# Channel attention: eight queries' exponentials made by ScalarE alone, with their keys innermost in memory, and the maxima formed in PSUM

## The chip, the cores and the metric

The kernel runs on one core of one Trainium2 chip. The metric is device time in microseconds for one launch, which works through all four batch elements. The engines are TensorE (PE, with its weight loads shown apart as PEld), VectorE (DVE), ScalarE (ACT), GpSimd (POOL) and SyncE (SP, which here only issues DMAs).

## What is computed

Four transformer layers follow one another on x of shape 4 x 512 x 128, each an attention and a feed-forward, each with a residual and a LayerNorm. The change touches the fourth attention, which attends over channels inside each token. For every token and each of 16 heads there are 64 queries, 64 keys and 64 values, all of them scalars:

```
Q = (x @ Wq + bq).reshape(b, s, 16, 64) / 8
K, V = the same from Wk, Wv (no scale)
scores = einsum('bshq,bshk->bshqk', Q, K)        # one product per (query, key)
scores = where(k > q, -inf, scores)              # causal over channels
w = softmax(scores, axis=-1)
attn = einsum('bshqk,bshk->bshq', w, V)
out = attn.reshape(b, s, 1024) @ Wo + bo
```

So a token has 16 x 64 x 64 / 2 scores and no matmul can make them. The first layer's feed-forward matters only because its weights (w1, w2, h1, h2, w3, 2.9 MB in all) move in memory.

## The kernel before, in words

Tokens lie on the 128 partitions, 128 of them at a time, so a batch element has four token tiles (`NT`). A loop runs the four batch elements; in each the channel stage comes seventh of eight and works through the four tiles one after the other. In it the 64 queries stand in reverse order (the last query, which sees all keys, first), and are cut into half 0 (the first 32 positions) and half 1 (the last 32).

The scores of a tile are cut into chunks of up to 2048 columns (`score_chunks`), each made of pieces of four keys by some queries by 16 heads, the head innermost. A tile has 20 chunks (`NC`): six of half 1 (`EARLY`), eight of half 0 with keys 0 to 31 (the rectangle), six of half 0 with keys 32 to 63. Chunk c of a tile is "step c" below. Each chunk passes through the engines in turn:

- POOL multiplies queries by keys (L1251) into one of five buffers `D3`;
- DVE subtracts the maximum of each query (`subtract`, L1287);
- ACT takes the exponential in place (L1235);
- PE adds the exponentials over keys by transposing each key's block onto an accumulating PSUM bank (`sum_keys`, L1170), the denominator `psD`;
- DVE multiplies the exponentials by the values into one of two buffers `W3` (`weigh`, L1300), and PE sums these too, the numerator `psA`.

The order of each engine is written out by hand. DVE's step n is: whatever is due at that step, then `subtract(n + 2)`, then `weigh(n)`. PE's step n is: the denominator of chunk n, then the numerator of chunk n-1. `weigh(n)` waits for the numerator of chunk n-2, since there are two buffers `W3`. What is due at certain steps on DVE: `scan_keys` (L1269, running maxima and minima over the keys of the next tile), `maxima` (L1278 to L1280, which turns these into the maximum of each query, since a score is a product of two scalars), `finish` (reciprocal L1308 and product L1312 of a half), `residual` (L1320). PE fills queries and keys of the next tile into one bank (`fill_qk`, L1141 and L1142), ACT moves them to SBUF (`move_qk`, L1222), and for keys writes a second, head-major copy (L1226). In the first tile of a batch element nothing of this is hidden.

Of the kernel before, what the change touches and what calls it, by code (L numbers as in the profile page):

```python
# [12 lines left out]
P = 128  # L13
BATCH, T = 4, 512
NT = T // P
HID = 512
# [15 lines left out]
CHUNK = 2048  # L32


def score_chunks():

    def triangle(k0):
        out, at = [[]], 0  # L40
        for j in range(0, HD // 2, KB):
            n = HD // 2 - j
            if at + KB * NH * n > CHUNK:
                out.append([])
                at = 0
            out[-1].append((k0 + j, KB, n, at))
            at += KB * NH * n
        return out

    early = [(1, c, True) for c in triangle(0)]  # L50
    rect = [(0, [(k, KB, HD // 2, 0)], False) for k in range(0, HD // 2, KB)]
    late = [(0, c, True) for c in triangle(HD // 2)]
    return early + rect + late


def transformer(nc, inp, out, last_stage=8):
    ctx = ExitStack()
    with ctx:
# [20 lines left out]
        w1_0 = sb("w1_0", HID)  # L79
        w2_0 = sb("w2_0", HID)  # L80
        wh_0 = [sb(f"wh{j}_0", NM * HID) for j in (1, 2)]
        w3_0 = sb("w3_0", NM * P)
# [36 lines left out]
        AR = 24576  # L119
        arena = sb("arena", AR)  # L120
        top = [0]

        def take(cols):
            a = arena[:, top[0]:top[0] + cols]
            top[0] += cols
            assert top[0] <= AR, top[0]
            return a


# [23 lines left out]
        TK = take(16)  # L153

# [21 lines left out]
        QX = take(NH * HD // 2)  # L176
        QN = take(NH * HD // 2)
        RD = QX
        AT = [take(NH * HD) for _ in range(2)]
        D3 = [take(CHUNK) for _ in range(5)]  # L180
        W3 = [take(CHUNK) for _ in range(2)]

# [21 lines left out]
        chunks = score_chunks()  # L204

# [15 lines left out]
        with nc.Block() as block:  # L221
# [16 lines left out]
            def _(act):  # L238
# [6 lines left out]
                load(w1_0[:], inp["L0_ffn_w1_w"])  # L245
                load(w2_0[:], inp["L0_ffn_w2_w"])
                for w, name in zip(wh_0, ("h1", "h2")):
                    load(tiles(w[:], HID), inp[f"L0_ffn_{name}_w"].rearrange("(k p) n -> p k n", p=P))
                load(tiles(w3_0[:]), inp["L0_ffn_w3_w"].rearrange("(k p) n -> p k n", p=P))
# [30 lines left out]
            def _(pool):  # L280
# [9 lines left out]
                pool.wait_ge(consts, 7 + NE)  # L290
# [55 lines left out]
            def _(pe):  # L346
                pe.wait_ge(consts, 12 + NE)
# [47 lines left out]
        w_in = [sem(f"w_in{j}") for j in range(NSLOT)]  # L395

# [9 lines left out]
        c3 = {k: sem(f"c3_{k}") for k in ("d", "e", "w", "den", "num", "attn", "proj", "qk", "qk_sb", "v", "kh", "prod", "chain", "rT")}  # L406
# [686 lines left out]
        EARLY = sum(ch[0] == 1 for ch in chunks)  # L1093
        LATE = next(c for c in range(EARLY, NC) if chunks[c][2])

        QK_AT = {EARLY + 1 + j: j for j in range(4)}
        LAG = 1
        PROJ_AT = EARLY + 5
        V1_AT = 3
        V0_AT = LATE + 2  # L1100
        FINISH_1, FINISH_0 = EARLY + 2, 2
        RESIDUAL, SCAN, MAX_1, MAX_0 = PROJ_AT + 1, PROJ_AT + 2, PROJ_AT + 3, NC - 2
        assert MAX_1 < MAX_0 and V0_AT < NC and FINISH_0 + 1 < EARLY

        def half_of(n):
            return chunks[n % NC][0]

        def pieces(n):
            return chunks[n % NC][1]

        def filled(n):
            k, nk, w, at = pieces(n)[-1]
            return at + nk * NH * w
# [5 lines left out]
        def keys_on(a, piece):  # L1119

            k, nk, w, at = piece
# [3 lines left out]
        def queries_on(a, piece):  # L1125

            k, nk, w, at = piece
            return a[:, 0:NH * w][:, None, :].to_broadcast([P, nk, NH * w])

        def qk_bank(tt, j):  # L1130
            return psum[:, 4 + j, :] if tt == 0 else scratch

        def fill_qk(pe, tt, j):

            ps = qk_bank(tt, j)
            w, row, c = (wq3, wk3)[j // 2], 32 * (j // 2), slice(j % 2 * 512, j % 2 * 512 + 512)
            if tt > 0:
                pe.wait_ge(c3["qk_sb"], 4 * tt + j)
                if j == 3:
                    pe.wait_ge(c3["kh"], 2 * tt + 1)  # L1140
# [17 lines left out]
        def sum_keys(ps, buf, n):  # L1158


            half, ragged = chunks[n % NC][0], chunks[n % NC][2]
            first_key = 0
            last_key = HD // 2 - 1 if half == 1 else HD - 1
            for k, nk, w, at in pieces(n):
                for j in range(nk):
                    seen = w - j if ragged else w
                    for f in range(0, seen, 8):
                        rows = NH * min(8, seen - f)
                        c = at + NH * (j * w + f)
                        last = nc.tensor.matmul(ps[half][0:rows, f * NH:f * NH + P], buf[:, c:c + rows], ident[:],  # L1170
                                                start=k + j == first_key and f == 0,
                                                stop=k + j == last_key and f + 8 >= seen,
                                                is_transpose=True, skip_group_check=True)
# [40 lines left out]
        def channel_act(act):  # L1214
# [14 lines left out]
            for j in range(4):  # L1229
                move_qk(0, j)  # L1230
# [258 lines left out]
```

## Time and profile before

| | |
|---|---|
| median of 3 runs | 4073.07 us (4064.61 to 4074.36) |
| the profiled execution's own time | 4083.43 us |
| its span in the trace | 4081.8 us |
| granted TensorE clock, mean | 0.878 of full speed |
| busy share: PE, DVE, ACT, POOL | 78%, 66%, 35%, 40% |

The profiled execution has 1.6 us around its span and lies 0.25% above the median. A busy share over the whole span mixes eight stages with different limits, so the stage is read by itself in the rows below. A granted clock of 1.00 is 2.4 GHz and 0.50 is 1.2 GHz.

### The profile page before, as it was taken

The numbers are of one execution on the slowest core, as the hardware profiler recorded it, in microseconds if no ns is written. First come the engines' busy times: TensorE is split into PE (matmuls) and PEld (weight loads), VectorE is DVE, ScalarE is ACT, GpSimd is POOL, SyncE is SP. The second block draws the span as 40 slices with busy tenths as digits, with TensorE's granted clock in tenths as the row PEclk, the third lists the DMA queues.
The fourth block names the chain that finished last, engine by engine and source line by source line (L and its number), as shares of the span: only waits on it lengthen the run. The fifth ranks groups of instructions, "written<-read, shape, count | busy, mean of one in ns | idle before, by whom it ended". The sixth has DMA issues, their size and how long they took to land. (4 is left out here: it accounts for less than half of the span.)

```text
span 4081.8 us, 46282 instructions
## 1 busy us (share of the span) xinstructions
PE 3185.8 (78%) x17780; PEld 2115.1 (52%) x17780; DVE 2696.1 (66%) x4249; ACT 1425.6 (35%) x2344; POOL 1627.7 (40%) x972
## 2 busy tenths in 40 slices
PE   4877977778787796877868778678887877778787
PEld 2444456665343445767525343666743544267673
DVE  3456389996256529999515643999941574499993
ACT  1435233233253423333325442333332543133332
POOL 0212077772021207777103121777800311277770
PEclk9989978889898897988989888898898988799888
DMA  3000100000100010000000001000001000100000
GB/s 117 1 1 1 54 1 1 1 1 21 35 1 0 1 54 1 1 1 1 26 29 1 1 9 46 1 1 1 1 26 29 1 1 16 39 1 1 1 1 29
DMA packets 62136, 56.52 MB, mean 14 GB/s; under 512 B 6171, under 2 KB 47539, under 8 KB 61766
## 3 DMA queue, kind: packets, MB, share of 16 engines
q1 hardware_dynamic: 52800, 44.62, 3.7%
q10 hardware_dynamic: 9094, 8.72, 0.7%
q8 instruction: 146, 2.39, 0.2%
q14 instruction: 96, 0.79, 0.1%
HBM read 52.28 MB, written 1.05 MB: 13 GB/s over the span
## 5 line engine op out<-in xcount | busy, mean ns | idle before, releaser
L1251 POOL TENSOR_TENSOR arena<-arena 128x2048 f32<-128x2048 f32 (+7 forms) x384 | 1320.3, 3473 | 452.0 <-DVE arena L1300 346.8
L1170 PE MATMUL psum<-ident,arena 128*128 128x128 f32 (+7 forms) x9216 | 1154.4, 290 | 406.0 <-DVE arena L1300 293.2
L1170 PEld LDWEIGHTS psum<-ident,arena 128*128 128x128 f32 (+7 forms) x9216 | 1093.5, 145 | 511.0 <-DVE arena L1300 317.6
L1235 ACT ACTIVATE arena<-arena 128x2048 f32<-128x2048 f32 (+2 forms) x320 | 530.2, 1662 | 964.9 <-DVE arena L1287 964.8
L1300 DVE TENSOR_TENSOR arena<-arena,psum 128x2048 f32<-128x2048 f32 (+7 forms) x384 | 631.4, 1659 | 18.9 <-PE psum L1170 18.9
L1287 DVE TENSOR_TENSOR arena<-arena,psum 128x2048 f32<-128x2048 f32 (+7 forms) x384 | 631.3, 1660 | 4.4 <-POOL arena L1251 1.8
L460 POOL TENSOR_TENSOR rstd<-veps,mhalf 128x4 f32<-128x4 f32 x32 | 32.4, 1011 | 1206.6 <-DVE veps L451 1206.6
L750 POOL TENSOR_SCALAR arena<-arena 128x512 f32<-128x512 f32 (+3 forms) x512 | 263.7, 532 | 591.4 <-DVE arena L722 591.4
L679 ACT ACTIVATE arena<-arena 128x512 f32<-128x512 f32 (+3 forms) x512 | 281.9, 552 | 268.5 <-DVE arena L717 268.1
L636 PE MATMUL psum<-ident,arena 128*128 128x128 f32 x1280 | 194.9, 297 | 147.9 <-ACT arena L690 88.4
L636 PEld LDWEIGHTS psum<-ident,arena 128*128 128x128 f32 x1280 | 149.2, 150 | 253.5 <-ACT arena L690 133.4
L957 PE MATMUL psum<-arena,stream 128*128 128x512 f32 x512 | 265.7, 601 | 3.4 <-DVE arena L1078 3.4
L974 PE MATMUL psum<-arena,stream 128*128 128x512 f32 x512 | 246.0, 605 | 0.0
L1074 DVE TENSOR_TENSOR arena<-arena,psum 128x512 f32<-128x512 f32 x128 | 88.0, 688 | 220.0 <-PE psum L974 220.0
L611 PE MATMUL psum<-arena 64*128 64x256 f32 (+3 forms) x1024 | 198.3, 495 | 27.4 <-DVE arena L712 22.8
L1078 DVE TENSOR_TENSOR arena<-arena 128x512 f32<-128x512 f32 x128 | 88.6, 692 | 181.0 <-ACT arena L1008 181.0
L653 PE MATMUL psum<-arena 128*64 128x128 f32 x2560 | 192.3, 295 | 0.4
L712 DVE CUSTOM_DVE_ANT_0 arena<-psum,cmask 128x384 f32<-128x384 f32 (+3 forms) x256 | 112.2, 487 | 116.7 <-PE psum L611 116.6
L1269 DVE TENSOR_TENSOR_SCAN arena<-first,arena 128x1024 f32<-128x1024 f32 x32 | 132.1, 4170 | 75.7 <-ACT arena L1226 75.7
L1006 ACT ACTIVATE arena<-psum 128x512 f32<-128x512 f32 x128 | 76.4, 597 | 274.2 <-PE psum L974 274.2
L653 PEld LDWEIGHTS psum<-arena 128*64 128x64 f32 x2560 | 147.6, 145 | 31.9 <-issue 30.5
L957 PEld LDWEIGHTS psum<-arena,stream 128*128 128x128 f32 x512 | 88.7, 189 | 141.7 <-issue 72.0
(201 smaller groups left out, 3538.8 us busy)
## 6 DMA issues: line engine op xcount, KB each, us to landing
stream<-in_L_ffn_W SPq DMA_DIRECT2D x160, 256.0 KB, 3.1
wh<-in_L_ffn_h_w ACTq DMA_DIRECT2D x2, 1024.0 KB
wa<-in_L_attn_W_attn ACTq DMA_DIRECT2D x1, 1536.0 KB
wq<-in_L_attn_Wq ACTq DMA_DIRECT2D x2, 512.0 KB
wo<-in_L_attn_Wo ACTq DMA_DIRECT2D x2, 512.0 KB
x<-in_L_attn_x SPq DMA_DIRECT2D x4, 256.0 KB, 3.7
out_x<-x SPq DMA_DIRECT2D x4, 256.0 KB, 2.3
w<-in_L_ffn_w_w ACTq DMA_DIRECT2D x3, 256.0 KB
```

The source lines that it names most:

```text
L611: last = nc.tensor.matmul(GS[t % 2][:, half, g.cols(j)], QA[r, p * T + g.i * P:p * T + (g.i + 1) * P], KA[r, p // A.share * T:p // A.share ...
L636: last = nc.tensor.transpose(GX[:, half, c:c + P], two(PRG[b % 4])[:, half, c:c + P], ident[:])
L653: last = nc.tensor.matmul(GO[b % 2][half * HD:(half + 1) * HD, j * P:(j + 1) * P], V[:, c:c + HD], pt[:, half, j * g.n + kt * P:j * g.n + ...
L679: nc.scalar.activation(pr, pr, ACT.Exp, bias=nb[:, u:u + 1], scale=HD ** -0.5, accum_out=rsum[:, u:u + 1]).then_inc(s["probs"], 1)
L750: nc.gpsimd.tensor_scalar(pr, pr, rinv[:, u:u + 1], 1.0, ALU.mult, ALU.mult).then_inc(s["scaled"], 1)
L957: nc.tensor.matmul(psO, slot[:, 2 * HID + m * P:2 * HID + (m + 1) * P], HR[n % 3], start=n == 0, stop=top2 and n == NE * NM - 1).then_inc( ...
L974: nc.tensor.matmul(up_bank(n, j), slot[:, j * HID + m * P:j * HID + (m + 1) * P], XS[e % 2], start=True, stop=True).then_inc(s["up"], 1)
L1170: last = nc.tensor.matmul(ps[half][0:rows, f * NH:f * NH + P], buf[:, c:c + rows], ident[:], start=k + j == first_key and f == 0, stop=k + ...
L1235: nc.scalar.activation(D3[n % 5][:, 0:cols], D3[n % 5][:, 0:cols], ACT.Exp).then_inc(s["e"], 1)
L1251: last = nc.gpsimd.tensor_tensor(of_piece(D3[n % 5], piece), q, keys_on(K3[tt % 2], piece), ALU.mult)
L1287: last = nc.vector.tensor_tensor(d, d, queries_on(psM[half_of(n)], piece), ALU.subtract)
L1300: last = nc.vector.tensor_tensor(of_piece(W3[n % 2], piece), of_piece(D3[n % 5], piece), keys_on(psV, piece), ALU.mult)
```

## The change

- Eight queries of half 0 (`OWN`, the positions 0 to 7) leave POOL's products and DVE's subtraction. For these, one ACT instruction for each query and head (`own_scores`, 128 a tile, 57 to 64 columns) computes exp(q * k - maximum) straight from the keys, with the query as the per-partition scale and the negated maximum `NB` as the per-partition bias. It reads the keys with a step of 16 elements and writes them side by side into `EA`, whose innermost dimension is the key. They are issued ten behind each chunk's exponential in steps 2 to 14.
- DVE weighs these exponentials in six pieces in the last three steps of a tile, and PE sums them there, 64 transposes for the denominator (read from `EA` with a step of 64 elements) and 64 for the numerator.
- Chunks hold at most 1536 columns; a tile has 18: six of half 1 in pieces of two keys, eight of the rectangle (24 queries), four behind it.
- The maxima are made with the query read from PSUM: two scalar_tensor_tensor instructions with one SBUF operand each and a maximum, in place of three instructions whose operands are all in SBUF. Keys are filled and moved ahead of queries. For half 0 of later tiles ACT first copies the queries to PSUM.
- `EA` reaches into the room of the first feed-forward's weights, which are therefore loaded again in each batch element, by SP behind the last expert's weights, and the block ends only once they have landed.

The core of the diff:

```diff
-CHUNK = 2048
+OWN = 8
+CHUNK = 3 * 512
...
+        def sum_own(ps, buf, first_key, keys):
+            for j in range(keys):
+                k = first_key + j
+                rows = NH * min(OWN, HD - k)
+                last = nc.tensor.matmul(ps[0][0:rows, 0:P], buf[:, j, 0:rows], ident[:],
+                                        start=False, stop=k == HD - 1, is_transpose=True, skip_group_check=True)
...
+                    for o in OWN_W.get(c, ()):
+                        k, nk = own_pieces[o]
+                        pe.wait_ge(s["own"], (tt + 1) * len(own))
+                        sum_own(psD, by_key(EA)[:, k:k + nk, :], k, nk).then_inc(s["own_den"], 1)
...
+            def own_scores(tt, c):
+                keys = K3[tt % 2].rearrange("p (k h) -> p h k", h=NH)
...
+                for r, h in OWN_AT[c]:
+                    j = r * NH + h
+                    nc.scalar.activation(EA[:, j * HD:(j + 1) * HD - r], keys[:, h, 0:HD - r], ACT.Exp, bias=NB[:, j:j + 1],
+                                         scale=Q3[tt % 2][:, j:j + 1]).then_inc(s["own"], 1)
...
-                nc.vector.tensor_tensor(high, mx, q[:, r, :], ALU.mult)
-                then(nc.vector.tensor_tensor(low, mn, q[:, r, :], ALU.mult))
-                then(nc.vector.tensor_tensor(psM[half], QX, QN, ALU.max))
+                nc.vector.scalar_tensor_tensor(low, m, by, mn, ALU.mult, ALU.mult)
+                then(nc.vector.scalar_tensor_tensor(m, m, by, mx, ALU.mult, ALU.mult))
+                then(nc.vector.tensor_tensor(psM[half], psM[half], QN, ALU.max))
+                if half == 0:
+                    if tt > 0:
+                        dve.wait_ge(s["own"], tt * len(own))
+                    nc.vector.tensor_scalar(NB, psM[0][:, 0:NH * OWN], -1.0, None, ALU.mult).then_inc(s["neg"], 1)
...
+                        e = EA.rearrange("p (q h k) -> p k q h", k=HD, h=NH)[:, k:k + nk]
+                        last = nc.vector.tensor_tensor(of_piece(buf, (k, nk, OWN, 0)), e, keys_on(psV, k, nk, OWN), ALU.mult)
...
+                    sp.wait_ge(nrm["xT"], 7)
+                    for dst, src in ffn0_weights:
+                        sp.dma_start(dst, src).then_inc(w0_in, 16)
...
+                    sp.wait_ge(w0_in, 16 * len(ffn0_weights))
```

On ACT, in the rectangle of the first tile of a batch element, exponentials (L1235) and the moves of the next tile (L1222, L1226) stood so before:

```order
L1235 ACTIVATE arena<-arena 128x2048 x3
L1222 ACTIVATE arena<-psum 128x512
L1235 ACTIVATE arena<-arena 128x2048
L1222 ACTIVATE arena<-psum 128x512
L1235 ACTIVATE arena<-arena 128x2048
L1222 ACTIVATE arena<-psum 128x512
L1226 ACTIVATE arena<-psum 128x32x16
```

The same place of the changed kernel (L1301 is a chunk's exponential, L1274 and L1278 the moves, L1291 the small ones):

```order
L1301 ACTIVATE arena<-arena 128x1536
L1274 ACTIVATE arena<-psum 128x512
L1278 ACTIVATE arena<-psum 128x32x16
L1291 ACTIVATE arena<-arena 128x60 x10
L1301 ACTIVATE arena<-arena 128x1536
L1274 ACTIVATE arena<-psum 128x512
L1278 ACTIVATE arena<-psum 128x32x16
L1291 ACTIVATE arena<-arena 128x59 x10
L1301 ACTIVATE arena<-arena 128x1536
```

Ten small exponentials now stand between one chunk's exponential and the next, behind the moves.

On DVE, the end of a tile before (L1287 subtracts, L1300 weighs, L1278 to L1280 are the maxima of half 0 of the next tile):

```order
L1300 TENSOR_TENSOR arena<-arena,psum 128x1280
L1278 TENSOR_TENSOR arena<-arena 128x512
L1279 TENSOR_TENSOR arena<-arena 128x512
L1280 TENSOR_TENSOR psum<-arena 128x512
L1287 TENSOR_TENSOR arena<-arena,psum 128x2048
L1300 TENSOR_TENSOR arena<-arena,psum 128x1024
L1300 TENSOR_TENSOR arena<-arena,psum 128x768
```

And in the changed kernel, steps 15 and 16 (L1371 subtracts, L1389 weighs, L1395 weighs pieces of the eight queries):

```order
L1371 TENSOR_TENSOR arena<-arena,psum 128x768
L1389 TENSOR_TENSOR arena<-arena,psum 128x1280
L1389 TENSOR_TENSOR arena<-arena,psum 128x256
L1395 TENSOR_TENSOR arena<-arena,psum 128x1536 x2
L1371 TENSOR_TENSOR arena<-arena,psum 128x1024
L1371 TENSOR_TENSOR arena<-arena,psum 128x512
L1389 TENSOR_TENSOR arena<-arena,psum 128x1024
L1389 TENSOR_TENSOR arena<-arena,psum 128x512
L1395 TENSOR_TENSOR arena<-arena,psum 128x1024
L1395 TENSOR_TENSOR arena<-arena,psum 128x1536
```

The maxima have left the end of the tile, and two weighings of the eight queries' exponentials stand in each of its last three steps.

On PE in the same two steps (L1198 are transposes of a chunk, L1211 those of the eight queries), from the denominator of chunk 15 on:

```order
L1198 MATMUL psum<-ident,arena 16x128
L1211 MATMUL psum<-ident,arena 128x128 x24
L1198 MATMUL psum<-ident,arena 128x128 x5
L1198 MATMUL psum<-ident,arena 112x128
L1198 MATMUL psum<-ident,arena 128x128 x2
L1198 MATMUL psum<-ident,arena 96x128
```

The 24 denominators of the eight queries stand ahead of the numerator of chunk 14, for which DVE's next weighing but one waits.

## Rows read from the trace of the kernel before

**Rows 1.** Windows, one stretch in the stage: engines PE, PEld, DVE, ACT, POOL, then clock.
```profile
640.00:750.00 110.00, 87.56 (x634) 75.43 (x634) 107.92 (x63) 37.38 (x27) 84.26 (x25) 0.91 0.00 1
```

**Rows 2.** DVE's timeline: half 0 finished, tiles 1, 2 and the last.
```profile
663.66 3.35 DVE L1308 RECIPROCAL arena<-psum 128x512 f32<-128x512 f32 x1
...
771.52 3.35 DVE L1308 RECIPROCAL arena<-psum 128x512 f32<-128x512 f32 x1
...
962.87 0.69 DVE L1312 TENSOR_TENSOR arena<-arena,psum 128x512 f32<-128x512 f32 x1
```

**Rows 3.** DVE's timeline: one step of the rectangle, then the two scans.
```profile
605.85 2.28 DVE L1287 TENSOR_TENSOR arena<-arena,psum 128x2048 f32<-128x2048 f32 x1
608.04 2.28 DVE L1300 TENSOR_TENSOR arena<-arena,psum 128x2048 f32<-128x2048 f32 x1
610.24 7.13 DVE L1269 TENSOR_TENSOR_SCAN arena<-first,arena 128x1024 f32<-128x1024 f32 x2
```

**Rows 4.** Groups by line: the maxima before, 32 of each.
```profile
L1279 DVE TENSOR_TENSOR arena<-arena 128x512 f32<-128x512 f32 x32 | 105.1, 3285 | 0.0
...
L1278 DVE TENSOR_TENSOR arena<-arena 128x512 f32<-128x512 f32 x32 | 81.1, 2536 | 0.3
...
L1280 DVE TENSOR_TENSOR psum<-arena 128x512 f32<-128x512 f32 x32 | 47.8, 1493 | 1.1
```

**Rows 5.** Timeline of DVE, and of POOL: maxima without POOL and beside it.
```profile
548.27 1.01 DVE L1279 TENSOR_TENSOR arena<-arena 128x512 f32<-128x512 f32 x1
...
621.54 1.03 DVE L1278 TENSOR_TENSOR arena<-arena 128x512 f32<-128x512 f32 x1
622.50 3.07 DVE L1279 TENSOR_TENSOR arena<-arena 128x512 f32<-128x512 f32 x1
...
621.71 5.49 POOL L1251 TENSOR_TENSOR arena<-arena 128x1024 f32<-128x1024 f32 x2 [6.49 <-DVE arena L1300]
```

**Rows 6.** Timeline: start of the stage in the first batch element.
```profile
514.41 0.60 ACT L1222 ACTIVATE arena<-psum 128x512 f32<-128x512 f32 x1 [3.41 <-PE psum L1142]
...
523.10 24.44 POOL L1251 TENSOR_TENSOR arena<-arena 128x2048 f32<-128x2048 f32 x6 [19.43 <-ACT arena L1222]
...
523.99 11.64 DVE L1269 TENSOR_TENSOR_SCAN arena<-first,arena 128x1024 f32<-128x1024 f32 x2 [18.92 <-ACT arena L1226]
...
550.04 5.88 DVE L1287 TENSOR_TENSOR arena<-arena,psum 128x2048 f32<-128x2048 f32 x3
```

**Rows 7.** ACT's groups by form: after the bar busy us and mean ns.
```profile
L1008 ACT ACTIVATE arena<-psum,b 128x512 f32<-128x512 f32 x128 | 88.0, 687 | 154.9 <-PE psum L979 154.9
...
L679 ACT ACTIVATE arena<-arena 128x128 f32<-128x128 f32 x128 | 49.5, 388 | 37.6 <-DVE arena L717 37.6
...
L1235 ACT ACTIVATE arena<-arena 128x1536 f32<-128x1536 f32 x32 | 47.6, 1486 | 120.5 <-DVE arena L1287 120.5
...
L1226 ACT ACTIVATE arena<-psum 128x512 f32<-128x512 f32 x32 | 34.7, 1086 | 0.0
```

**Rows 8.** PE's timeline: transposes in a row, then one fill's second half.
```profile
676.58 12.01 PE L1170 MATMUL psum<-ident,arena 128*128 128x128 f32 x108
...
701.28 1.12 PE L1142 MATMUL psum<-bqkv,ones 1*128 1x512 f32 x2
```

**Rows 9.** PEld's groups by form: weight loads of 128 and of 16 columns.
```profile
L1170 PEld LDWEIGHTS psum<-ident,arena 128*128 128x128 f32 x7424 | 930.1, 151 | 509.8 <-DVE arena L1300 317.6 <-issue 169.1 <-ACT arena L1235 10.5
...
L1170 PEld LDWEIGHTS psum<-ident,arena 128*16 128x16 f32 x256 | 23.8, 93 | 0.8
```

**Rows 10.** Windows behind a scan, columns as in rows 1.
```profile
726.00:732.00 6.00, 2.47 (x12) 2.47 (x13) 6.00 (x4) 1.70 (x1) 2.45 (x1) 0.57 0.00 0
620.00:626.00 6.00, 4.32 (x20) 4.28 (x21) 5.96 (x4) 1.16 (x1) 4.29 (x2) 0.50 0.00 0
```

**Rows 11.** SP's waits, and a window of the first loads (last column GB/s).
```profile
SPq L1363 <- DVE x L454: 108.8, 4, 27.3
...
10.00:20.00 10.00, 0.70 (x2) 0.37 (x2) 3.83 (x16) 0.00 (x0) 0.00 (x0) 1.00 1.13 340
```

More of the change, by code:

```diff
@@ L1 @@
+from collections import namedtuple
 from contextlib import ExitStack
@@ L31, with pack @@
 KB = 4
-CHUNK = 2048
+OWN = 8
+CHUNK = 3 * 512
+Chunk = namedtuple("Chunk", "half first_query ragged pieces cols")
 def score_chunks():
[L39 to L53, printed above, removed]
+    def pack(half, first_query, ragged, keys, starts):
+        at, out = 0, []
+        for k in starts:
+            w = HD // 2 - first_query - (k % (HD // 2) if ragged else 0)
+            out.append((k, keys, w, at))
+            at += keys * NH * w
+        assert at <= CHUNK
+        return Chunk(half, first_query, ragged, out, at)
+    early = [pack(1, 0, True, 2, starts) for starts in ((0, 16), (2, 14), (4, 12), (6, 10), (8, 18, 22), (20, 24, 26, 28, 30))]
+    rect = [pack(0, OWN, False, KB, (k,)) for k in range(0, HD // 2, KB)]
+    late = [pack(0, OWN, True, KB, starts) for starts in ((32,), (36, 52), (40, 48), (44,))]
+    return early, rect, late
 def transformer(nc, inp, out, last_stage=8):
@@ L125, in take @@
             top[0] += cols
-            assert top[0] <= AR, top[0]
+            assert top[0] <= AR + LENT, top[0]
             return a
+        w1_0 = take(HID)
+        w2_0 = take(HID)
+        wh_0 = [take(NM * HID) for _ in range(2)]
+        w3_0 = take(NM * P)
+        top[0] = 0
         mx = take(NH * NT)
@@ L153, in transformer @@
         TK = take(16)
+        assert top[0] <= AR
         top[0] = 0
@@ L244, in _ @@
                 load(wvo0[:], inp["L0_attn_VO"])
[L245 to L249, printed above, removed]
+                for dst, src in ffn0_weights:
+                    load(dst, src)
                 for j, name in enumerate(("w1", "w2", "h1", "h2")):
@@ L1092, in transformer, with w_count, chunk_w @@
         NALL = NT * NC
[L1093 to L1113, printed above, removed]
+        EARLY, LATE = len(early), len(early) + len(rect)
+        Q0_AT, MAX_0, FINISH_0, V1_AT = 0, 1, 3, 3
+        PROJ_AT, RESIDUAL, FINISH_1 = EARLY, EARLY + 1, EARLY + 2
+        FILL_AT = {EARLY + 2 + j: j for j in range(4)}
+        MOVE_AT = {c + 1: j for c, j in FILL_AT.items()}
+        SCAN, MAX_1 = EARLY + 6, EARLY + 8
+        V0_AT = NC - 1
+        own = [(r, h) for r in range(OWN) for h in range(NH)]
+        OWN_AT = {c: own[10 * (c - 2):10 * (c - 1)] for c in range(2, NC - 3)}
+        assert sum(len(o) for o in OWN_AT.values()) == len(own)
+        own_pieces = [(0, 12), (12, 12), (24, 8), (32, 12), (44, 12), (56, 8)]
+        OWN_W = {NC - 3: (0, 1), NC - 2: (2, 3), NC - 1: (4, 5)}
+        by_step = [[("chunk", c)] + [("own", o) for o in OWN_W.get(c, ())] for c in range(NC)]
+        in_order = [item for step in by_step for item in step]
+        NW = len(in_order)
+        def w_count(tt, item):
+            return tt * NW + in_order.index(item) + 1
+        def chunk_w(n):
+            return w_count(n // NC, ("chunk", n % NC))
         def of_piece(buf, piece):
@@ L1156, in project_out, with sum_chunk, by_key @@
             last.then_inc(s["proj"], 1)
[L1158 to L1164, printed above, removed]
+        def sum_chunk(ps, buf, n):
+            ch = chunks[n % NC]
+            first = n % NC in (0, EARLY)
+            for k, nk, w, at in ch.pieces:
                 for j in range(nk):
-                    seen = w - j if ragged else w
+                    seen = w - j if ch.ragged else w
                     for f in range(0, seen, 8):
                         rows = NH * min(8, seen - f)
[L1169 to L1173, printed above, removed]
+                        c, to = at + NH * (j * w + f), NH * (ch.first_query + f)
+                        last = nc.tensor.matmul(ps[ch.half][0:rows, to:to + P], buf[:, c:c + rows], ident[:],
+                                                start=first, stop=False, is_transpose=True, skip_group_check=True)
+                        first = False
+            return last
+        def by_key(a):
+            return a.rearrange("p (n k) -> p k n", k=HD)
+        def sum_own(ps, buf, first_key, keys):
[4 more added lines that the diff above has]
+                                        start=False, stop=k == HD - 1, is_transpose=True, skip_group_check=True)
             return last
```

186 lines of the change are left out of this document (118 added, 68 removed).

## The prediction

> **What bounds the kernel now.** I read a window inside the channel stage first, since the page's shares mix eight stages. DVE is busy 107.9 of 110 us, PE 87.6, POOL 84.3, ACT 37.4 [rows 1]. The same instruction of two neighbouring tiles starts 107.86 us apart [rows 2], so DVE sets the period. Its instructions can be added up. 2048 columns take 2.2 us from start to start [rows 3] and three of 5376 columns together 5.8 [rows 6]: 1.042 ns a column and 0.067 us each. A tile subtracts and weighs 34816 columns in 24 pieces: 2 x 37.9 = 75.8 us. Scans take 7.2 [rows 3], the maxima 234.0 / 16 = 14.6 [rows 4], two reciprocals 6.8, their products, the residual and the like 1.7. That makes 106.1, and 1.8 is waiting.
>
> **What leaves DVE.** 26368 columns in 30 pieces remain: 2 x 29.5 = 58.9 us.
>
> *Maxima.* Alone, such an instruction takes 1.0 us, beside POOL 3.1 [rows 5]: the first started 0.17 us ahead of POOL's, the next met it. The new ones have one SBUF operand, as subtract and weigh do, and those keep 2.2 us while POOL runs [rows 1, 3]. So I price them at their time alone: 0.96 + 0.96 + 0.66 = 2.6 a half, 5.4 with `NB`; bounds are 3.0 if everything ran at the contiguous rate and 14.6 if the contention stayed. The Trainium skill, "SBUF — State Buffer", section "Who interferes with whom", says that a DVE instruction with two SBUF inputs contends with GpSimd and one with at most one does not; the trace agrees.
>
> *The start of a batch element.* The scans start at 523.99, behind the second key copy, and run beside POOL for 11.6 us; the first subtraction starts at 550.04 [rows 6]. Now keys are filled first: the second key half is moved at 514.4 instead of 522.4 [rows 6], its copy is done at 516.0, and POOL still waits for the queries until 523. The scans then run alone. I take 4.6 us (2.3 each, as alone; 7.2 would still end by 523.2). The maxima need the last queries (523.0) and end at 528.7. That is 21.3 us less in each batch element, the surest gain.
>
> **What is added.** *DVE weighs 8192 columns of the eight queries* with a step of 64 elements. A maximum alone reads with such a step: 0.96 us from start to start, so 1.74 ns a column [rows 5]. Six pieces: 14.7 us (8.9 if the step were free). DVE's tile: 58.9 + 14.7 + 7.2 + 5.4 + 8.5 = 94.7 us, 13.2 less than now, if it never waits.
>
> *ACT.* A small exponential has two pointer operands. One with one pointer and 128 columns takes 0.388 us [rows 7]; 67 columns fewer at 0.84 ns (the slope to 1486 ns for 1536 columns) take off 0.06; a pointer costs 0.09 (0.69 against 0.60) [rows 6, 7], and successive ones overlap by 0.09. So 0.33 us each if the step of 16 elements is free. The only stepped access of ACT is the key copy, a write: 1.09 us for 512 columns against 0.60 [rows 6, 7], or 0.9 ns a column. Sixty of these make 0.385. I take 0.385, since both DVE's reads and ACT's writes pay for a step. A step of ACT is then 10 x 0.385 + 1.4 = 5.25 us, while DVE needs 3.4 for subtract and weigh. All of ACT's work of a tile is only 79 us, but the order matters. `weigh(k)` needs exponential k. Count from the moment `NB` is ready (DVE's step 1). ACT finishes exponential 10 at 8 x 5.25 + 1.6 (a key move) = 43.2. DVE would want it at 40.1: nine steps of 3.3 to 3.5 us (30), two finishes of 4.1, the residual, and one subtraction; exponential 11 comes at 50.0 and is wanted at 46.5. Then the scans give ACT room. So 6.6 us of new waiting in tiles 1 and 2 of a batch element, 11 in the first (no finish ahead of it) and 9.5 in the last (no scans or maxima to hide in).
>
> *PE, the last three steps.* The 576 transposes of a tile are as many as before, but 128 of them now gather where DVE has least to do. A transpose takes 0.111 us at full clock [rows 8]. Loading 128 columns of weights costs 58 ns more than 16 [rows 9], 0.5 ns a column, hidden under the matmul. For the denominator of the eight queries every column is 256 bytes from the last. No row shows this; bounds are 0.111 (free) and 128 x 1.74 = 0.22 (DVE's price). I take 0.19, nearer the upper, since DVE and ACT both pay about 1.7 ns a column when stepping although their own rates differ. The Trainium skill, "Advanced Engine Details and Errata", section "SBUF Cachelines", says that accesses which each fall into another 16-byte line pay a penalty; it gives no time for it, and it speaks against keys innermost.
>
> Count from T, the end of `weigh(14)`. Exponential 15 is ready at T+0.4. PE: denominator of chunk 15 (16 transposes) 1.8, 24 of the eight queries 4.6, numerator 14 1.3: T+8.1, and only then may DVE's first piece start (wanted at T+2.6). It ends at 10.9. PE: 12 + 20 + 16 transposes, T+15.0; the second piece runs 15.0 to 17.8. Subtract, weigh and the next piece to 23.1; the fourth waits for the numerator of chunk 16 (8 + 20 + 12 transposes behind T+19.1) until 25.1, and ends at 27.9. The sixth waits for PE (values' fill 2.0, then 20 transposes) until 33.4 and ends at 35.3. DVE's own work there is 23.4, so it waits 11.9; with free loads the same count gives 30.2 and 6.8. PE idles 5 us just before, and behind such a gap the granted clock is 0.57 and 0.50, with 20 transposes in 4.3 us [rows 10]: 1.7 more. Tile: 94.7 + 6.6 + 13.6 = 114.9, or 7.1 more than now.
>
> *Hidden.* POOL loses a quarter of its columns, and its 84 us lie under the period [rows 1]. The first weights, 2.9 MB, are issued behind the last expert's; SP idles 27.3 us there before the output [rows 11], and the first loads ran at 340 GB/s, so some 9 us. GpSimd's memset lies in the start-up's wait for weights.
>
> **The sum for a batch element,** against finishes of half 0 at 663.66, 771.52, (879.4) and 963.6 [rows 2]. Start -21.3; the first tile pays 11 and its tail 13.6 and more, so that its finish comes at about 658, -5.6 in all. Tiles 1 and 2: +7.1 each. The last: 57.7 to T, 36.1 of tail (exponential 15 comes at T+2.8, but no fill follows), 5.0 to the finish: 98.8 against 84.2, +14.6. Together +23, four times +93. In the profiled execution 4083 + 93 = 4176; against the median, 0.25% less, **4166 us**.
>
> **Rivals.** (1) *ACT's stepped reads are free*, 0.33 us each. Its step is 4.7 us; waits shrink by 4.5 a tile, 9 and 6.6 in the first and last, and T+0.4 becomes T-2.3, 2.7 more. That is 35 a batch element, 142 in all: 4024 us, faster than before. It decides from 0.35 us a piece on. For it: only a write shows the penalty on ACT. Against: DVE's reads show one. Chance 0.20. (2) *PE's stepped loads are free*, 0.111: 5 us less a tile, in all about 4088. PE loads at another rate than DVE reads, and the load may hide under the matmul. 0.18. (3) *Both free:* 3946; 0.08. (4) *DVE's step is free too and nothing waits*, so its columns alone decide: 88.9 and a few us of waits a tile, about 3850. Rows 5 speak against it. 0.04. (5) *The clock stays at half through the tail:* 140 transposes at 0.216 instead of 0.111 add 14.7 us a tile, less the 1.7 counted, about 4370. Against: once busy, PE kept 0.111 us over 108 transposes [rows 8]. 0.06. My forecast keeps 0.44.
>
> **How the numbers follow.** The forecast's own range is 4110 to 4230: loads at 0.15 to 0.22, ACT's pieces at 0.37 to 0.41. The whole range, 3980 to 4235, takes in rivals 1 and 2 and leaves out 3, 4, 5 and a tail, about 0.2. A change of 0.3%, 12 us, is about what can be told from none. Slower: nearly all of the forecast (0.42), half of rival 2 (0.09), rival 5 (0.06): 0.57. The same: 0.08, mostly rival 2. Faster: rivals 1, 3, 4 and a sliver: 0.35.
>
> **What would show it.** The first subtraction of a batch element 21 us earlier; the maxima near 1.0, 1.0 and 0.7 us beside POOL; small exponentials at 0.38 us from start to start (0.33: rival 1); DVE waiting for the chunk exponential around steps 10 and 11; weight loads of the eight queries' denominator clearly longer than 151 ns and PE pairs at 0.19 (0.11: rival 2); DVE waiting for PE at its first, second and fourth piece; a tile of about 115 us; 0.96 us for 512 stepped columns. Wrong it would be above all through ACT's 0.385, worth 2.6 us per ns over the launch.

## The result, and the profile after

The changed kernel takes 4144.42 us (median of 4 runs, 4142.11 to 4148.86) where the kernel before took 4073.72 (4064.61 to 4077.43) beside it: ratio 1.0178, 95% interval 1.0159 to 1.0197. It is slower by 71 us. The forecast was 4166, which is 22 us more than was measured. The two profiled executions are 61.4 us apart (4143.2 us of span against 4081.8), where the forecast had added up 93. The mean clock is 0.902.

The window of [rows 1], in the changed kernel:

```profile
640.00:750.00 110.00, 85.03 (x595) 70.63 (x594) 93.57 (x80) 77.72 (x153) 64.76 (x30) 0.95 0.00 1
```

DVE, busy 107.9 of 110 us before, is busy 93.6, and still a tile has become longer: over this window no engine is full, each waits for another. Where DVE waits is in its timeline. First the start of the first batch element, then the maxima of half 0 of the second tile and the finish of half 0 in tiles 1 and 2 (in brackets the idle time ahead and what ended it):

```profile
516.79 4.47 DVE L1342 TENSOR_TENSOR_SCAN arena<-first,arena 128x1024 f32<-128x1024 f32 x2 [10.89 <-ACT arena L1278]
...
529.65 1.21 DVE L1371 TENSOR_TENSOR arena<-arena,psum 128x1024 f32<-128x1024 f32 x1
...
644.31 1.05 DVE L1357 SCALAR_TENSOR_TENSOR arena<-psum,arena 128x512 f32<-128x512 f32 x1
645.27 1.07 DVE L1358 SCALAR_TENSOR_TENSOR psum<-psum,arena 128x512 f32<-128x512 f32 x1
646.37 0.70 DVE L1359 TENSOR_TENSOR psum<-psum,arena 128x512 f32<-128x512 f32 x1
...
654.28 3.36 DVE L1404 RECIPROCAL arena<-psum 128x512 f32<-128x512 f32 x1
...
766.77 3.36 DVE L1404 RECIPROCAL arena<-psum 128x512 f32<-128x512 f32 x1
```

The first subtraction starts 20.4 us earlier than in [rows 6]. The maxima cost 2.8 us a half instead of 7.3 [rows 4]. But the same finish is now 112.49 us apart, against 107.86 in [rows 2]. Between the two lie the new waits, in steps 10 and 11 and behind them in the last three steps:

```profile
691.86 1.75 DVE L1389 TENSOR_TENSOR arena<-arena,psum 128x1536 f32<-128x1536 f32 x1 [2.83 <-ACT arena L1301]
...
698.34 1.75 DVE L1389 TENSOR_TENSOR arena<-arena,psum 128x1536 f32<-128x1536 f32 x1 [3.06 <-ACT arena L1301]
...
717.88 1.75 DVE L1389 TENSOR_TENSOR arena<-arena,psum 128x1536 f32<-128x1536 f32 x1
...
725.99 2.82 DVE L1395 TENSOR_TENSOR arena<-arena,psum 128x1536 f32<-128x1536 f32 x1 [3.76 <-PE psum L1198]
731.96 2.78 DVE L1395 TENSOR_TENSOR arena<-arena,psum 128x1536 f32<-128x1536 f32 x1 [3.15 <-PE psum L1198]
...
741.24 2.77 DVE L1395 TENSOR_TENSOR arena<-arena,psum 128x1536 f32<-128x1536 f32 x1 [1.20 <-PE psum L1198]
...
751.51 1.92 DVE L1395 TENSOR_TENSOR arena<-arena,psum 128x1024 f32<-128x1024 f32 x1 [2.16 <-PE psum L1198]
```

5.9 us of waiting for ACT and 10.3 for PE in this tile. In the list of DVE's waits over the whole launch (us, times, longest) these are

```profile
DVE arena L1395 <- PE psum L1198: 161.3, 60, 5.0
...
DVE arena L1389 <- ACT arena L1301: 106.2, 44, 3.1
```

267.5 us together; [rows 1] leave DVE 2.1 us idle of 110. What PE does in those last steps, in its timeline (L1198 are transposes of a chunk, L1211 those of the eight queries):

```profile
719.16 1.96 PE L1198 MATMUL psum<-ident,arena 128*128 128x128 f32 x16 [1.56 <-ACT arena L1301]
720.96 3.68 PE L1211 MATMUL psum<-ident,arena 128*128 128x128 f32 x24
724.48 2.78 PE L1198 MATMUL psum<-ident,arena 128*128 128x128 f32 x24
727.10 3.07 PE L1211 MATMUL psum<-ident,arena 128*128 128x128 f32 x20
...
734.79 1.53 PE L1211 MATMUL psum<-ident,arena 128*128 128x128 f32 x12 [1.56 <-DVE arena L1395]
...
744.07 2.29 PE L1211 MATMUL psum<-ident,arena 128*128 128x128 f32 x12 [1.99 <-DVE arena L1395]
```

From start to start, 24 stepped transposes take 3.52 us (0.147 each), 24 others 2.62 (0.109). And PE in turn waits 1.56 and 1.99 us for a piece that DVE began at 731.96 and 741.24, about a microsecond before PE came to it: the two hand the two buffers `W3` to and fro. PE has the larger part of the work here. From 720 to 753 us it is busy 29.2 of 33 us and DVE 22.7, and the two waits are nearly all that PE lacks.

The clock is 1.00 in the four windows of 6 us from 716 to 740, and up to 753 it falls once, behind the 1.99 us of idling:

```profile
746.00:748.00 2.00, 2.00 (x5) 0.49 (x3) 2.00 (x2) 1.26 (x1) 1.32 (x1) 0.50 0.00 0
```

Last ten small exponentials of ACT in a row, the groups of these (one of the eight forms), of the stepped weighing and of PE's weight loads for the eight queries (busy us, mean ns of one), and the 24 stepped loads behind 720.8 us by themselves (shortest, median and longest ns):

```profile
678.49 3.97 ACT L1291 ACTIVATE arena<-arena 128x61 f32<-128x61 f32 x10
...
L1291 ACT ACTIVATE arena<-arena 128x64 f32<-128x64 f32 x256 | 103.0, 488 | 38.9 <-DVE arena L1363 38.9
...
L1395 DVE TENSOR_TENSOR arena<-arena,psum 128x1536 f32<-128x1536 f32 x64 | 178.9, 2796 | 144.9 <-PE psum L1198 141.9 <-PE psum L1211 3.0
...
L1211 PEld LDWEIGHTS psum<-ident,arena 128*128 128x128 f32 x1824 | 242.8, 202 | 88.1 <-DVE arena L1395 86.9
...
L1211 PEld LDWEIGHTS psum<-ident,arena x24: 225/260/266, 720.9 to 724.2; 128*128 128x128 f32 x24
```

Successive exponentials overlap: the ten take 3.81 us until ACT's next instruction starts (682.30), 0.381 each; all 2048 are busy 809.8 us, 0.395 each. The mean of 202 ns for L1211 mixes two kinds, since its denominators are read from `EA` with a step and its numerators from `W3` side by side: a stepped load takes 260 ns, one of the others 141 (median of 23 from 731.6 us on). SP still idles 24.6 us before the output (27.3 in [rows 11]), and no wait of SP for the weights shows in the trace.

### The profile page after: what moved, and what is told of

Read it like the earlier page. It is cut to its first block and busy times, and to the rows that moved or that the text cites. A ratio compares the mean times of both kernels' runs of the same rounds, so it can differ in the third digit from the quotient of the medians.

```text
span 4143.2 us, 48799 instructions
## 1 busy us (share of the span) xinstructions
PE 3242.3 (78%) x17780; PEld 2135.6 (52%) x17780; DVE 2493.5 (60%) x4553; ACT 2076.3 (50%) x4372; POOL 1336.4 (32%) x1069
## 5 line engine op out<-in xcount | busy, mean ns | idle before, releaser
L1324 POOL TENSOR_TENSOR arena<-arena 128x1536 f32<-128x1536 f32 (+9 forms) x480 | 1025.1, 2164 | 670.0 <-DVE arena L1389 567.0
L1198 PE MATMUL psum<-ident,arena 128*128 128x128 f32 (+7 forms) x7168 | 932.9, 290 | 333.5 <-ACT arena L1301 255.9
L1198 PEld LDWEIGHTS psum<-ident,arena 128*128 128x128 f32 (+7 forms) x7168 | 842.5, 144 | 456.3 <-ACT arena L1301 285.1
L1291 ACT ACTIVATE arena<-arena 128x64 f32<-128x64 f32 (+7 forms) x2048 | 809.8, 503 | 38.9 <-DVE arena L1363 38.9
L1301 ACT ACTIVATE arena<-arena 128x1536 f32<-128x1536 f32 (+2 forms) x288 | 412.0, 1443 | 359.8 <-DVE arena L1371 359.3
L1389 DVE TENSOR_TENSOR arena<-arena,psum 128x1536 f32<-128x1536 f32 (+9 forms) x480 | 495.4, 1067 | 120.6 <-ACT arena L1301 106.2
L1371 DVE TENSOR_TENSOR arena<-arena,psum 128x1536 f32<-128x1536 f32 (+9 forms) x480 | 494.7, 1065 | 8.2 <-POOL arena L1324 6.3
L1211 PE MATMUL psum<-ident,arena 128*128 128x128 f32 (+6 forms) x2048 | 292.1, 296 | 74.3 <-DVE arena L1395 74.3
L1395 DVE TENSOR_TENSOR arena<-arena,psum 128x1536 f32<-128x1536 f32 (+1 forms) x96 | 240.2, 2505 | 164.3 <-PE psum L1198 161.3
L1211 PEld LDWEIGHTS psum<-ident,arena 128*128 128x128 f32 (+6 forms) x2048 | 265.2, 195 | 88.7 <-DVE arena L1395 86.9
L442 ACT ACTIVATE xT<-psum 128x512 f32<-128x512 f32 x32 | 19.1, 598 | 457.5 <-PE psum L436 457.5
```

Source lines behind the costliest of these rows:

```text
L1198: last = nc.tensor.matmul(ps[ch.half][0:rows, to:to + P], buf[:, c:c + rows], ident[:], start=first, stop=False, is_transpose=True, skip_g ...
L1211: last = nc.tensor.matmul(ps[0][0:rows, 0:P], buf[:, j, 0:rows], ident[:], start=False, stop=k == HD - 1, is_transpose=True, skip_group_ch ...
L1291: nc.scalar.activation(EA[:, j * HD:(j + 1) * HD - r], keys[:, h, 0:HD - r], ACT.Exp, bias=NB[:, j:j + 1], scale=Q3[tt % 2][:, j:j + 1]).t ...
L1301: nc.scalar.activation(D3[n % 5][:, 0:cols], D3[n % 5][:, 0:cols], ACT.Exp).then_inc(s["e"], 1)
L1324: last = nc.gpsimd.tensor_tensor(of_piece(D3[n % 5], piece), q, keys_on(K3[tt % 2], k, nk, w), ALU.mult)
L1371: last = nc.vector.tensor_tensor(d, d, queries_on(psM[ch.half], ch, piece), ALU.subtract)
```

## The experiments

Each ratio is against the kernel before, run on the same chip; 0.01 is 41 us. The difference of two ratios is uncertain by about 0.003. Besides, the kernel before itself took 4086.77 and 4088.05 us beside four and two of the runs and 4073.20 beside the other three, while 4073.72 stood beside the changed kernel, which was run only there. So a difference of ratios can be some 13 us off. The traces have a steadier measure, the channel stage, from ACT's first move of queries or keys to DVE's last `residual` (us, sum of the four batch elements, each in its profiled execution):

| kernel | stage | against the changed kernel |
|---|---|---|
| before | 1812.0 | |
| changed | 1867.9 | |
| the gaining half alone, two runs | 1607.9, 1607.8 | -260.0 |
| ACT reads without a step | 1742.1 | -125.8 |
| key outermost | 1766.3 | -101.6 |
| PE without a step | 1822.5 | -45.4 |
| numerators first | 1839.9 | -28.0 |
| both store orders | 1658.0 | -209.9 |
| both, and PE's order | 1659.1 | -208.8 |
| both, spread out | 1700.9 | -167.0 |

All else in the launch takes 2269 to 2275 us in every one of them.

**The half that gains, alone.** Before's chunks, POOL and DVE take all 64 queries, nothing is loaded again; what stays is the maxima in PSUM and keys filled ahead of queries.

```diff
-CHUNK = 3 * 512
+CHUNK = 2048
-        OWN_AT = {c: own[10 * (c - 2):10 * (c - 1)] for c in range(2, NC - 3)}
-        OWN_W = {NC - 3: (0, 1), NC - 2: (2, 3), NC - 1: (4, 5)}
+        OWN_AT = {}
+        OWN_W = {}
...
-                    for dst, src in ffn0_weights:
-                        sp.dma_start(dst, src).then_inc(w0_in, 16)
```

> The chunks of the kernel before (20 of up to 2048 columns, all 64 queries through POOL, DVE and ACT), with only the other half of the change: maxima from queries in PSUM, keys filled and moved first. No eight queries apart, no weights loaded again. If the gain of the change is what I said, it stands here alone: 21.3 us at the start of a batch element and 9 us in each of three later tiles (14.6 to 5.6 for the maxima), four times 48 = 194, so about 3880 us. Rival: what DVE no longer spends is waited for on PE (88 of 110 us busy) or POOL (84); then about 4000.

Measured: 3880.08 us, ratio 0.9504 (0.9486 to 0.9523). Its timelines of POOL and DVE show the maxima beside POOL, and its window DVE full again:

```profile
614.33 20.90 POOL L1319 TENSOR_TENSOR arena<-arena 128x2048 f32<-128x2048 f32 x8 [1.41 <-PE psum L1193]
```
```profile
631.01 1.06 DVE L1352 SCALAR_TENSOR_TENSOR arena<-psum,arena 128x512 f32<-128x512 f32 x1
631.99 1.06 DVE L1353 SCALAR_TENSOR_TENSOR psum<-psum,arena 128x512 f32<-128x512 f32 x1
...
640.82 3.35 DVE L1393 RECIPROCAL arena<-psum 128x512 f32<-128x512 f32 x1
...
738.28 3.35 DVE L1393 RECIPROCAL arena<-psum 128x512 f32<-128x512 f32 x1
```
```profile
640.00:750.00 110.00, 92.11 (x694) 77.57 (x693) 109.62 (x71) 41.37 (x30) 91.66 (x28) 0.97 0.00 1
```

POOL runs from 614.3 to 635.2, and one with a single SBUF operand takes 1.06 us within it, where 3.07 stood in [rows 5]. A tile takes 97.46 us. So the eight queries, with their chunks and the weights loaded again, cost 1.0178 - 0.9504 = 0.067, and 260 us by the stages: the change is a gain of 5% with a loss of over 6% on top.

**ACT reads the keys without a step.** The head-major copy of the keys gets two buffers, and ACT reads from it. (To make room, the reciprocals share the buffer `QN`.)

```diff
-        KH = take(NH * HD)
+        KH = [take(NH * HD) for _ in range(2)]
-                keys = K3[tt % 2].rearrange("p (k h) -> p h k", h=NH)
+                keys = KH[tt % 2].rearrange("p (h k) -> p h k", h=NH)
```

> The changed kernel with ACT reading the keys of the eight queries from the head-major copy, side by side (a second copy buffer, no other change). My theory: the step costs 0.05 to 0.06 us of a piece, so 0.395 becomes 0.34; DVE's 106 us of waiting for a chunk's exponential nearly vanish and exponential 15 comes earlier, in all about 4030 us. Rival: the piece costs what it does for its fixed part (two pointers), whatever the step: still 0.39 us and 4144 us.

Measured: 4016.85 us, ratio 0.984 (0.982 to 0.986). The group of the same form, and DVE's waits:

```profile
L1291 ACT ACTIVATE arena<-arena 128x64 f32<-128x64 f32 x256 | 88.1, 426 | 39.0 <-DVE arena L1363 39.0
```
```profile
DVE arena L1395 <- PE psum L1198: 131.6, 60, 5.0
...
DVE arena L1389 <- ACT arena L1301: 38.8, 28, 2.5
```

By busy time the piece fell from 0.40 to 0.344 us, 2048 of them by 117 us in all; from start to start ten take 3.30 us instead of 3.81. DVE waits 67 us less for ACT, 30 less for PE before it weighs and 19 less for PE before `residual`. The kernel gained 0.034, and 126 us by the stages. The step in ACT's reads cost near what rival 1 had given for it (142).

**The eight queries' exponentials stored with the key outermost.** Now ACT writes with a step of 128 elements, and DVE and PE read side by side.

```diff
-                    nc.scalar.activation(EA[:, j * HD:(j + 1) * HD - r], keys[:, h, 0:HD - r], ACT.Exp, bias=NB[:, j:j + 1],
+                    nc.scalar.activation(by_key(EA)[:, 0:HD - r, j], keys[:, h, 0:HD - r], ACT.Exp, bias=NB[:, j:j + 1],
-                        e = EA.rearrange("p (q h k) -> p k q h", k=HD, h=NH)[:, k:k + nk]
+                        e = EA.rearrange("p (k q h) -> p k q h", k=HD, h=NH)[:, k:k + nk]
```

> The changed kernel with the exponentials of the eight queries stored with the key outermost: ACT writes with a step of 128 elements, DVE and PE read side by side. My theory: DVE's 8192 columns fall from 14.7 to 8.9 us a tile (2.80 to 1.67 us for 1536) and PE's loads from 0.146 to 0.111 us, some 5 us a tile after the waits on PE, 80 in all, about 4065 us, if ACT pays for reading and writing with a step only once (0.395 us a piece as now). Rival: the two steps add up on ACT (0.45 us a piece); then the waits for exponentials grow by 5 us a tile and the time stays near 4144.

Measured: 4040.33 us, ratio 0.989 (0.9869 to 0.991). Its groups on ACT, DVE and PEld:

```profile
L1291 ACT ACTIVATE arena<-arena 128x64 f32<-128x64 f32 x256 | 102.8, 492 | 38.9 <-DVE arena L1363 38.9
```
```profile
L1395 DVE TENSOR_TENSOR arena<-arena,psum 128x1536 f32<-128x1536 f32 x64 | 112.2, 1753 | 139.6 <-PE psum L1198 136.6 <-PE psum L1211 3.0
```
```profile
L1211 PEld LDWEIGHTS psum<-ident,arena 128*128 128x128 f32 x1824 | 201.8, 141 | 40.8 <-DVE arena L1395 39.6
```

A piece of DVE lost 1.04 us, the mean load 61 ns, which is some 120 for each that had been stepped, and ACT, which now steps in reading and in writing, pays nothing more. It gained 0.029, and 102 us by the stages.

**PE's stepped loads by themselves.** PE takes its denominators side by side from `EA`, and so sums other elements, which gives false denominators; DVE keeps its step.

```diff
-                        sum_own(psD, by_key(EA)[:, k:k + nk, :], k, nk).then_inc(s["own_den"], 1)
+                        sum_own(psD, tiles(EA)[:, k:k + nk, :], k, nk).then_inc(s["own_den"], 1)
```

> The changed kernel, except that PE reads the eight queries' exponentials for the denominator side by side, 128 columns in a row, instead of with a step of 64 (these are other elements, so their denominators are wrong; ACT and DVE do what they did). It prices PE's stepped load by itself. My theory: its transposes fall from 0.146 to 0.111 us, 64 x 0.035 = 2.2 us of PE a tile where DVE waits for PE, so 1.5 to 2 us a tile, 25 to 35 us in all: ratio to the kernel before about 1.010 where the changed kernel had 1.018. Rival: the loads are hidden under other work and the ratio stays 1.018.

Measured: 4096.92 us, ratio 1.0058 (1.0034 to 1.0081). Its PE timeline and loads:

```profile
608.50 2.78 PE L1211 MATMUL psum<-ident,arena 128*128 128x128 f32 x24
611.12 2.78 PE L1198 MATMUL psum<-ident,arena 128*128 128x128 f32 x24
```
```profile
L1211 PEld LDWEIGHTS psum<-ident,arena 128*128 128x128 f32 x1824 | 207.6, 144 | 84.2 <-DVE arena L1395 82.8
```

2.62 us for 24, the same as any other. The step costs 0.012, and 45 us by the stages, or 2.8 a tile. 64 transposes by 0.037 us are 2.4, so all of it lies on the path. If the two parts add up, the 102 us of the other store order are 45 from PE and 56 from DVE; DVE's part was not run alone.

**PE takes the numerator of the chunk before first,** and the eight queries' denominators behind it, so that a buffer `W3` comes free earlier.

```diff
+                if n > 0:
+                    weighed(pe, n - 1)
                 if n < NALL:
                     for o in OWN_W.get(c, ()):
...
-                if n > 0:
-                    weighed(pe, n - 1)
```

> The changed kernel with PE's order in the last three steps changed: the numerators of the step before first, then the denominators of the eight queries. My theory: DVE's first piece waits for 24 denominators (3.5 us) for the order's sake alone; its waits on PE (161 us in all) fall by about 70 us, about 4075 us. Rival: PE's work in the tail is the bound, whatever its order; the waits move to the third piece and to the finish, and the time stays within 15 us of 4144.

Measured: 4111.11 us, ratio 1.0066 (1.0046 to 1.0086). The four of DVE's six pieces of a tile that wait:

```profile
720.37 3.02 DVE L1396 TENSOR_TENSOR arena<-arena,psum 128x1536 f32<-128x1536 f32 x1 [0.27 <-PE psum L1198]
726.93 2.78 DVE L1396 TENSOR_TENSOR arena<-arena,psum 128x1536 f32<-128x1536 f32 x1 [3.54 <-PE psum L1198]
...
736.45 2.77 DVE L1396 TENSOR_TENSOR arena<-arena,psum 128x1536 f32<-128x1536 f32 x1 [1.44 <-PE psum L1198]
...
747.79 1.92 DVE L1396 TENSOR_TENSOR arena<-arena,psum 128x1024 f32<-128x1024 f32 x1 [3.24 <-PE psum L1198]
```

The first wait is gone, 3.76 to 0.27, but the last grew from 2.16 to 3.24, and 8.5 of 10.3 us are left. It gained 0.011, but only 28 us by the stages, and not the 70 that I had expected: over the launch these waits fell from 161.3 to 139.7 us, and the ones of `residual` from 33.3 to 27.6.

**Both store orders at once:** ACT reads side by side and writes stepped, DVE and PE read side by side. The diff is the two above together.

> Both single edits together: ACT reads the keys of the eight queries side by side, and writes the exponentials with the key outermost. If the gains add up (0.029 for the store order, 0.034 for ACT's read): ratio 0.955. Rival A: ACT's stepped write costs what its stepped read did, a piece stays at 0.395 us, and the ratio is that of keys_outer alone, 0.989. Rival B: both relieve the same waits on PE at the end of a tile; then 0.970.

Measured: 3931.64 us, ratio 0.9652 (0.9627 to 0.9676). The piece of ACT, and DVE's waits:

```profile
L1291 ACT ACTIVATE arena<-arena 128x64 f32<-128x64 f32 x256 | 90.1, 486 | 39.0 <-DVE arena L1363 39.0
```
```profile
DVE arena L1395 <- PE psum L1198: 137.5, 60, 4.1
...
DVE arena L1389 <- ACT arena L1301: 39.0, 28, 2.5
...
DVE rT L1416 <- PE psum L1182: 14.2, 4, 3.7
```

0.352 us with a stepped write, 0.344 with no step, and 0.40 both with a stepped read and with two steps. By ratios the gains fall short of adding up, 0.965 where 0.955 was expected, but most of this is the kernel before, which was slower beside the single edits. By the stages they give 125.8 + 101.6 = 227, and 210 came. Part of the 17 us that are lacking is in DVE's waits for PE: 137.5 us, more than the 131.6 with ACT's change alone.

**The same, and PE's order too.**

> keys_outer_contig with PE's numerators first in the last three steps. If it adds up (0.011 more): 0.944 under the first theory, 0.978 under rival A. What matters: whether the eight queries apart can beat the same maxima without them (max_only, 0.950). My theory says only if ACT's piece falls to 0.34 us in spite of its stepped write.

Measured: 3931.36 us, ratio 0.965 (0.9625 to 0.9675): nothing. With dear transposes the order was worth 28 us, with cheap ones it is worth none. From 700 to 732 us PE is busy 28.92 of 32 us without the new order and 28.74 with it; most of what is left is spent waiting for DVE. So near the end of a tile PE's own work is close to being the limit, as the rival in the expectation for PE's order alone had it.

**Spread out.** On top of the two store orders, the exponentials in steps 1 to 13, and eight pieces of eight keys, two in each of the last four steps.

```diff
-        OWN_AT = {c: own[10 * (c - 2):10 * (c - 1)] for c in range(2, NC - 3)}
-        OWN_W = {NC - 3: (0, 1), NC - 2: (2, 3), NC - 1: (4, 5)}
-        own_pieces = [(0, 12), (12, 12), (24, 8), (32, 12), (44, 12), (56, 8)]
+        OWN_AT = {c: own[10 * (c - 1):10 * c] for c in range(1, NC - 4)}
+        OWN_W = {NC - 4 + i: (2 * i, 2 * i + 1) for i in range(4)}
+        own_pieces = [(8 * o, 8) for o in range(8)]
```

> keys_outer_contig with the eight queries' sums spread over four steps instead of three: ten small exponentials in each of steps 1 to 13, eight pieces of eight keys, two in each of steps 14 to 17. It tests whether what still separates it from max_only is that 128 transposes gather where DVE has least to do. There DVE waited 137 us for PE and 39 us for exponentials. My theory: with 56 transposes (6.2 us) against 5.7 us of DVE in such a step, the waits on PE fall by half or more, 70 to 80 us: ratio 0.945 to 0.948, level with or just below max_only (0.950). Rival: DVE waits for the order (two buffers of weighted exponentials), not for PE's amount of work, so as many waits stay, only shorter pieces of each: 0.960 to 0.966.

Measured: 3972.09 us (median of 5), ratio 0.9719 (0.9706 to 0.9733), worse than what it started from, by 43 us in the stages, and beyond what either theory had given. DVE's waits, and the group of the first small exponentials:

```profile
DVE arena L1395 <- PE psum L1198: 123.4, 64, 3.6
...
DVE arena L1389 <- ACT arena L1301: 62.3, 48, 2.5
DVE rT L1416 <- PE psum L1182: 49.7, 16, 3.7
```
```profile
L1291 ACT ACTIVATE arena<-arena 128x64 f32<-128x64 f32 x256 | 90.0, 485 | 118.5 <-DVE arena L1363 118.5
```

The pieces were not what made it worse: DVE's waits for a buffer fell by 14 us, though they are as many as before (every second piece waits, 0.5 to 2.6 us). The waits for exponentials grew by 23 us and those of `residual` by 35.5, which with 4 us of longer weighing is more than the whole loss. Both point at the early start on ACT. In step 1 the negated maximum is not ready, ACT stands 118.5 us for it (39.0 before), and the chunks' exponentials behind it come late. At 658.3 us PE waits 1.70 us for one of them, with the projection behind it, for which `residual` then waits 2.93 us at 664.64. The two halves of this edit were not run apart, so this is read from the trace and not shown by a run.

**The gaining half once more,** unedited, beside the run above.

> The same kernel as max_only, beside spread on one chip, so that the two can be told apart: ratio 0.949 to 0.952, no new mechanism.

Measured: 3884.54 us (median of 5), ratio 0.9505 (0.9492 to 0.9519). This is the fastest version, by 5% against the kernel before and over 6% against the changed one, and faster by 0.015 than the best form of the eight queries.

## Why the prediction was right

**The gaining half** is the surest. Its maxima took 1.06 us each beside POOL, 2.8 a half where 2.6 was predicted, so the price "at their time alone" held, and the start came 20.4 us earlier (21.3 predicted). Alone it was expected to give 194 us; the kernel before beside it took 4086.77 and not 4073, so it gave 207 (204 by the stages), and that it came to the expected 3880 us exactly is luck.

**ACT.** The places were right (steps 10 and 11), with 5.9 us where 6.6 was predicted, and so was the mechanism: the step in its reads, worth 0.034, was by itself the difference between slower and faster, as rival 1 had it. The piece took 0.381 us from start to start against 0.385. But its reason was wrong by half, and that the number fits is partly luck: I had taken the price from a stepped write (0.9 ns a column). A stepped read costs 0.05 us of a piece of 64 columns, and a stepped write 0.01 or less.

**PE's tail.** The count from T (the end of `weigh(14)`, where DVE's next instruction starts, 719.54) can be held against the trace:

| start of piece | predicted | measured |
|---|---|---|
| 1 | T+8.1 | T+6.4 |
| 2 | T+15.0 | T+12.4 |
| 4 | T+25.1 | T+21.7 |
| 6 | T+33.4 | T+32.0 |

The pieces that wait were the ones predicted, for 10.3 us instead of 13.6 a tile. Two terms make the difference. The one that was mis-sized is "I take 0.19": a stepped transpose takes 0.147 us, nearer the lower bound of 0.111, so rival 2 was half right, and 64 of them by 0.043 are 2.8 us. And exponential 15 came 0.8 us earlier than T+0.4: PE starts on it at 719.16. Only the mean of DVE's and ACT's price had spoken for 0.19. The load itself takes even more than the prediction's upper bound, 0.260 us against 0.22; successive loads overlap, so that only 0.038 us more of its 0.12 shows in a transpose.

The clock's 1.7 us came at another place than predicted. Ahead of the first piece PE idled 1.56 us and not 5, and the clock was 1.00. It fell to 0.50 behind the 1.99 us of idling that end at 744.07, where 12 transposes took 2.08 us (1.31 at 0.109 each) and the fill of the values 2.9 (2.0 predicted): again 1.7 us, and the reason why piece 6 is only 1.4 us ahead of the count where piece 4 was 3.4 ahead.

**The sum.** In the first batch element half 0 is finished at 654.28, 766.77, 879.26 and (970.17 from the start of its reciprocal) 974.3 us. The prediction's 658, then 114.9 a tile, then 98.8, gives 658, 772.9, 887.8 and 986.6. Each tile came in 2.4 us under, the first and the last 3.7 and 3.8. A tile: 3.3 from the tail, 0.7 from ACT, 0.6 from the scans (6.6 us, not 7.2), less 1.5 that no term had, a wait of the residual for PE; 0.7 stay unaccounted for. The first tile's -5.6 holds some 4 us ("and more") that its terms do not give: -21.3 - 13.2 + 11 + 13.6 is -9.9, and -9.4 was measured.

Over the launch these 12.3 us an element would take 49 off the 93. In return 1.7 us an element came behind the last half, where the residual waits 3.96 us for PE (2.2 before), and the kernel before was shorter in its second and third element than in the first, by 6.8 and 2.8 us, which makes the change dearer there. In the stages the change costs 11.6, 18.5, 14.3 and 11.5 us. The prediction had counted before's third tile at 107.86 us; its finish stood at 883.43 and not at 879.4, which only shifts 4 us between two terms.

**Where a gain went.** By the prediction's count DVE had 13.2 us less work a tile, and the trace shows 14 in 110. All of it and 4.6 more went into waits. No engine is full over a tile, but its last three steps give PE and DVE 128 transposes and six pieces on top, through two buffers, and there PE is busy 29.2 of 33 us. PE's order moved these waits and hardly lessened them; making the pieces cheaper did, as far as 97.97 us for the second tile (643.91 to 741.88 in the version with both store orders; its third takes 99.3), against the 97.46 of the gaining half alone.

That version still loses 0.015 to the gaining half, and by the stages 50 us or 12.5 a batch element: 3.2 in the first three tiles and 9.8 in the last (85.7 us from half 0's finish to the residual against 75.9) in its first one. That the last tile has no fill, scan or maxima of a next one to cover ACT and PE is a reading, not shown by a run. Whether the order through two buffers holds the rest or PE's work does stays open: the two were not told apart, and a third buffer `W3` was not tried. The reloaded weights, POOL and the memset were hidden, as predicted: outside the stage, the versions with weights and memset take no longer than those without, and DVE waits for POOL's products 6.3 us in the whole launch (1.8 before).

## What to carry to other kernels

Two changes in one can hide each other: here a 5% gain came together with a loss of over 6%, and only the run of the gaining half alone showed it. Moving work from a full engine to an idle one pays by what the consumers then wait for, so count from the moment the last producer is ready, and price the layout once for every engine that touches it: side by side for those who read most, with the step on the side that pays least. And when the reference itself varies, compare the stage that was changed in the traces, not only two ratios.

## What the runs showed of the hardware that was not expected

- **A step costs each engine and side differently.** DVE about 1.74 ns a column instead of 1.04 when it reads (2796 against 1753 ns for 1536), ACT 0.05 us of a piece of 64 columns when it reads and 0.01 or less when it writes, PE 0.12 us a load (0.260 against 0.141), of which 0.038 shows in a transpose. On ACT a stepped read and a stepped write together cost no more than the read (0.40 us both times). So a write of 512 columns from PSUM (1086 ns against 600, [rows 6, 7]) says little of short ones.
- **The kernel before loses some 4 us in some tiles at a lower clock.** In the third tile its PE ran at 0.50 of full speed and DVE waited; in the second, with the same instructions, at 0.87 and it didn't:

```profile
674.00:680.00 6.00, 6.00 (x35) 3.67 (x34) 6.00 (x4) 1.93 (x1) 6.00 (x2) 0.87 0.00 0
...
782.00:788.00 6.00, 6.00 (x16) 2.92 (x15) 6.00 (x4) 1.91 (x1) 6.00 (x2) 0.50 0.00 0
```
```profile
792.06 1.02 DVE L1300 TENSOR_TENSOR arena<-arena,psum 128x512 f32<-128x512 f32 x2 [3.96 <-PE psum L1170]
```

Before it PE had stood idle for 4.07 us, in the second tile for 3.07. Its second batch element had no such wait and took 6.8 us less than its first; the four of the changed kernel agree within 0.3 us.
